# A spectral filter's coefficients laid out channel by channel: eviction into a staging tile, copies on POOL

## The chip, the cores and the metric

The kernel runs on one core of one Trainium2 chip. The metric is device time in microseconds of one execution: the median of several runs of the same kernel. A profiled execution gives the trace; it has a time of its own, and a span from its first to its last instruction.

Five engines work side by side, each on its own queue of instructions: PE (TensorE, the matrix multiplier; its weight loads are shown as PEld), DVE (VectorE), ACT (ScalarE), POOL (GpSimd) and SP, which here only issues DMAs. They meet in semaphores: an instruction adds to one when it is done, and another engine's queue waits until it has reached a count.

## What is computed

The input x is 32 images of 16 x 16 tokens with 32 channels, all in fp32. Four layers follow each other, each a pair of a mixing block and a feed-forward block on a normalised input, added back: linear attention and a spectral filter bank (layer 0), a triangle product and a recurrent cell (1), a row scan and a mixture of experts (2), a row scan and a recurrent cell (3). The change touches the filter bank of layer 0 and, in time, the attention that runs beside its preparation:

```python
def _stu_conv(phi, u, n):                      # u: (b, 256, 32), phi: (1024, 16)
    Vf = jnp.fft.rfft(phi, n=n, axis=0)
    Uf_p = jnp.fft.rfft(u, n=n, axis=1)
    Uf_m = jnp.fft.rfft(u * sgn3, n=n, axis=1)
    U_plus = jnp.fft.irfft(Vf[None, :, :, None] * Uf_p[:, :, None, :], n=n, axis=1)[:, :sl]
    U_minus = jnp.fft.irfft(Vf[None, :, :, None] * Uf_m[:, :, None, :], n=n, axis=1)[:, :sl]
    return U_plus, U_minus * sgn[None, :, None, None]
...
for i, frac in enumerate((1, 2, 4, 8)):        # the first T, T/2, T/4, T/8 tokens
    xi = x[:, :T // frac]
    si = einsum('btkd,k,kde->bte', U_plus, s, Mpp) + einsum('btkd,k,kde->bte', U_minus, s, Mpm) + ar(Mu, xi)
    outs.append(pad(si))
return jnp.sum(jnp.stack(outs, axis=-1) * weights, axis=-1)
```

## The kernel before

The program is written engine by engine: one function each for `sync`, `gpsimd`, `tensor`, `scalar` and `vector`, and the order of every queue is the order of the code. There is no scheduler. `S("name")` is a semaphore.

**Attention, 16 rounds.** `U = 16` pairs of a token chunk and an image group pass through a software pipeline. The loops `for i in range(U + 3)` on PE and ACT hold round i: ACT takes the exponential of the shifted q of unit i - 1 (`a_q`, L1226), the transposed k (`a_kn`, L1232), the exponential of k of unit i (`a_k`, L1211), then v (`a_v`, L1220). DVE turns the sum of the exponential of q into weights (L1534, L1536, L1539). POOL's `q_normalise(u)` (L591) multiplies exponential and weights of unit u; since the exponential of unit u comes in round u + 1, so does this product. Matmuls go through the helper `full` (L646).

**Filter turns.** Beside the rounds 6 to 13 the filters of the spectral bank are made, two turns a round: `filter_turn(i, part)` gives turn m = 2 (i - 6) + part, 16 in all. Turn m makes the output channels m and m + 16. PE writes them into banks 4 and 5 (`filters(m)`; it first waits for `filt_sb >= m`, the eviction of the turn before), and ACT evicts them in three instructions (`a_filters(m)`): short filters in time (L1240), spectra `w_f[1]` of the half-length filter on 64 partitions (L1242), and spectra `w_f[0]` of the full-length filter on 128 partitions (L1244). Each of the two spectra is 2 channels x 256 values: 128 frequencies, real and imaginary part. On ACT the first turn of a round lies ahead of `a_v`, the second behind it.

**How the spectra lie.** A partition is an input channel of a part of the filter. In the tiles `w_f` the 256 x 32 values of a partition are laid out as (n, e, i) with `FI = 8` values i of neighbouring frequencies side by side, then the 32 channels e, then the blocks n of frequencies. An eviction writes runs of 8 floats; a read of one frequency's 32 channels steps 8 floats.

**The filter stage.** After attention PE transforms the tokens, and `frequencies` multiplies, frequency by frequency: the weights are the spectrum of x at one frequency (32 columns, `x_fb`), the moving operand is 2 x 32 values of `w_fr`. A call has 128 such matmuls, four of them side by side on four column groups, and a matmul in fp32 leaves two records in the trace. The first call uses `w_f[0]`, the second `w_f[1]`. Between them stand `segment` (L846), which reads the Toeplitz tile `toep` that SP's DMAs fill out of the short filters, and `way_back` (L870), the inverse transform.

Of the kernel before, what the change touches and what calls it, by code (L numbers as in the profile page):

```python
# [21 lines left out]
P = 128  # L22
# [32 lines left out]
HT = T // 2  # L55
FREQ = HT
LAGS = T // 4
FI = 8
TRI_ORDER = [2, 3, 0, 1]
DFT_BANKS = [6, 7, 0, 1, 2, 5, 3, 7]  # L60

# [39 lines left out]
def build(nc, force_steps=False, **d):  # L101
    x, out = d["x"], d["out"]
    with ExitStack() as ctx:
# [64 lines left out]
        SEG_T = [None, None, T // 4, T // 8]  # L168
        SEG_AT = [None, None, 0, T // 4]
        toep = arena[:, AT_TOEP:AT_TOEP + N_TOEP].rearrange("p (t e) -> p t e", e=C)  # L170

# [368 lines left out]
        @block.sync  # L542
        def _(sp):
            def load(name, dst, src):
                sp.dma_start(dst, src).then_inc(S(name), 16)

            load_x(sp, 0, (0, 1))
            load("consts_in", consts[:, :], d["consts"])
            load_x(sp, 1, (0, 1))
            load("w_attn_in", w_attn[:, :], d["w_attn"])  # L550
            for to, rows in FILTER_ROWS:
                load("w_stu_in", w_stu[to:to + rows.stop - rows.start, :], d["w_stu"][rows, :])
            for to, rows in FILTER_ROWS:
                load("w_spec_in", wm_raw[to:to + rows.stop - rows.start, :, :].rearrange("p f m -> p (f m)"), d["w_spec"][rows, :])
            load("w_fft_in", arena[:, AT_FFT:AT_FFT + N_FFT], w_fft)
            load("w_late_in", w_late[:, :], d["w_late"])


            sp.wait_ge(S("filt_zero"), 1)
            sp.wait_ge(S("filt_sb"), C // 2)  # L560
            for n in (3, 2):
                for r in range(NQ):
                    sp.dma_start(toep[C * r:C * r + C, SEG_AT[n]:SEG_AT[n] + SEG_T[n], :],
                                 filt[C * n:C * n + C, AR - r:AR - r + SEG_T[n], :]).then_inc(S(f"toep{n}_in"), 16)
            sp.wait_ge(S("back_f"), 3)
            for par in range(2):
                load("w_moe", w1[64 * par:64 * par + C + 1, :, :],
                     d["w1"].rearrange("(e two) d h -> two d e h", two=2)[par])
            load("w_moe", w2[:, :, :], d["w2"][:, 0:HID, :].rearrange("e h o -> h e o"))
            store_first(sp, (0, 1))  # L570
            sp.wait_ge(S("y_final"), 2)
            store_last(sp, (0, 1))
            sp.wait_ge(S("stored"), 16 * 2 * NQ)
# [3 lines left out]
        def _(pool):  # L577
# [23 lines left out]
            for u in range(U):  # L601
                q_normalise(u)
                if 2 <= u < 2 + FRACS - 1:
                    pool.wait_ge(S("wm_scaled"), u)
                    link(pool.tensor_tensor(wm_raw[:, u - 1, :], wm_raw[:, u - 1, :], wm_raw[:, u - 2, :], ALU.add))
                if u == FRACS:
                    pool.sem_inc(S("wm_seg"), 1)


            pool.wait_ge(S("stu_ps"), 1)  # L610
# [31 lines left out]
        def _(pe):  # L642
# [234 lines left out]

            pe.wait_ge(S("x_f_act"), 4)
            pe.wait_ge(S("x_f_dve"), 4)
            frequencies(0, slice(0, P), w_fr[0])  # L880
            segment(2, 8, 16).then_inc(S("stu_ps"), 1)

# [284 lines left out]
        def _(act):  # L1167
# [70 lines left out]
            def a_filters(m):  # L1238
                act.wait_ge(S("filt_ps"), m + 1)
                act.activation(filt[2 * C:, AR:, m::C // 2].rearrange("p t e -> p e t"),  # L1240
                               bank[2 * C:, 4:6, 2 * FREQ:2 * FREQ + LAGS], ACT.Copy)
                act.activation(w_f[1][0:2 * C, m::C // 2, :, :],  # L1242
                               bank[0:2 * C, 4:6, 2 * FREQ:4 * FREQ].rearrange("p k (n i) -> p k n i", i=FI), ACT.Copy)
                act.activation(w_f[0][:, m::C // 2, :, :],  # L1244
                               bank[:, 4:6, 0:2 * FREQ].rearrange("p k (n i) -> p k n i", i=FI), ACT.Copy)\
                    .then_inc(S("filt_sb"), 1)

            for i in range(U + 3):
                if 0 <= i - 1 < U:
# [759 lines left out]
```

## Time and profile before

| | us |
|---|---|
| median of 3 runs (384.47 to 387.49) | 385.49 |
| profiled execution | 385.72 |
| its span, first to last instruction | 383.9 |
| PE busy | 346.4 |
| VectorE busy | 229.1 |
| ScalarE busy | 191.1 |
| POOL busy | 31.9 |

A sum over parts of the trace is made against the profiled execution's 385.72. Busy time is the sum of an engine's instructions; matmuls are pipelined, so PE's records overlap, and how fast PE works is read from the distance between starts. Rows of a timeline merge neighbours of one kind, with their count behind an x.

### The profile page before, as it was taken

The page shows a single profiled execution, that of the slowest core. Times are in us where ns is not written, and L with a number is a line of the kernel's source. Part 1 is how long each engine was busy: PE and PEld are TensorE (multiplying, and loading weights), DVE is VectorE, ACT ScalarE, POOL GpSimd, SP SyncE. Part 2 cuts the span into 40 slices and gives each one's busy share as a digit, 9 for nine tenths or more (in the row PEclk, how much of TensorE's full clock was granted, in tenths as well). Part 3 has the DMA queues.
Part 4 walks back from the last instruction along what each step waited for, and adds up shares of the span by engine and source line. Part 5 has one row for each costly group of instructions (what it writes and reads, how often), then busy time and mean ns, then how long its engine had stood idle before and what let it go on. Part 6 is the DMA issues. An engine that isn't in the chain of part 4 may idle for free.

```text
span 383.9 us, 9504 instructions
## 1 busy us (share of the span) xinstructions
PE 346.4 (90%) x4064; PEld 231.1 (60%) x4064; DVE 229.1 (60%) x461; ACT 191.1 (50%) x419; POOL 31.9 (8%) x37
## 2 busy tenths in 40 slices
PE   7967999999998999998988999799998899999990
PEld 2434555655645799974655369247746654773790
DVE  2679967767766522137846773762437366245884
ACT  1959678979748500026672646360247315033560
POOL 0024722121220000000000000000000000000000
PEclk9999999999999999999999999899999899999996
DMA  8982000000330000002000000000000000000004
GB/s 238 155 161 87 2 2 3 2 3 3 87 81 0 3 3 2 5 22 36 2 2 2 0 3 0 3 0 2 2 0 2 0 3 0 2 2 1 2 0 112
DMA packets 7338, 9.91 MB, mean 26 GB/s; under 512 B 3694, under 2 KB 6398, under 8 KB 6910
## 3 DMA queue, kind: packets, MB, share of 16 engines
q1 hardware_dynamic: 5630, 8.23, 10.3%
q10 hardware_dynamic: 1664, 1.05, 1.0%
q8 instruction: 33, 0.54, 0.6%
q14 instruction: 11, 0.09, 0.1%
HBM read 6.65 MB, written 1.05 MB: 20 GB/s over the span
## 4 chain that ended last, share of the span: by engine, by line
PE 64%; DVE 15%; ACT 13%; issue 5%; DMA 2%; SPq 0%; DVEq 0%; ACTq 0%
PE bank L646 28%; PE bank L1076 6%; PE bank L274 6%; PE bank L268 5%; PE bank L1006 4%; PE bank L1017 4%; PE bank L846 2%; ACT lnv L373 2%; PE bank L870 2%; DMA sb_consts<-in_consts 2%; ACT rs L378 2%; ACT arena L1242 1%; ACT arena L1244 1%; DVE arena L1771 1%; PE bank L1133 1%
## 5 line engine op out<-in xcount | busy, mean ns | idle before, releaser
L367 ACT ACTIVATE sq<-bank 128x512 f32<-128x512 f32 x33 | 19.4, 591 | 66.1 <-PE bank L268 50.7
L646 PE MATMUL bank<-xn,sb_w_attn 128*128 128x512 f32 x64 | 34.6, 622 | 6.8 <-ACT attn_scratch L1211 4.3
L646 PE MATMUL bank<-sb_consts 128*128 128x512 f32 (+1 forms) x84 | 37.4, 554 | 0.0
L274 PE MATMUL bank<-sq,sb_consts 128*128 128x512 f32 x66 | 34.7, 611 | 0.6 <-ACT sq L367 0.3
L373 ACT ACTIVATE lnv<-bank 128x512 f32<-128x512 f32 x33 | 19.7, 597 | 30.2 <-PE bank L274 29.9
L646 PE MATMUL bank<-arena 64*32 64x256 f32 (+4 forms) x466 | 26.7, 382 | 3.6 <-ACT arena L1244 2.2
L1076 PEld LDWEIGHTS bank<-arena,sb_w_late 128*128 128x128 f32 x180 | 23.0, 190 | 10.8 <-DVE arena L1829 7.6
L1017 PE MATMUL bank<-arena,sb_w_late 128*128 128x128 f32 x144 | 27.9, 276 | 0.0
L1006 PE MATMUL bank<-arena,sb_consts 128*128 128x128 f32 x144 | 27.7, 276 | 0.1
L1076 PE MATMUL bank<-arena,sb_w_late 128*128 128x128 f32 (+1 forms) x180 | 26.4, 283 | 1.4 <-DVE arena L1813 0.2
L1384 ACT ACTIVATE arena<-bank 128x128 f32<-128x128 f32 x72 | 20.0, 278 | 13.9 <-PE bank L1017 13.7
L646 PEld LDWEIGHTS bank<-arena 64*32 64x32 f32 (+3 forms) x466 | 17.4, 167 | 14.0 <-ACT arena L1244 8.2
L591 POOL TENSOR_TENSOR attn_scratch<-attn_scratch 128x512 f32<-128x512 f32 x16 | 20.4, 1275 | 62.4 <-DVE attn_scratch L1539 62.4
L646 PE MATMUL bank<-arena,attn_scratch 128*32 128x128 f32 (+2 forms) x768 | 24.0, 294 | 0.6 <-DVE attn_scratch L1584 0.6
L1829 DVE SCALAR_TENSOR_TENSOR arena<-bank,xn 128x128 f32<-128x128 f32 x30 | 8.8, 292 | 26.1 <-PE bank L1076 25.4
L646 PEld LDWEIGHTS bank<-arena,attn_scratch 128*32 128x32 f32 (+1 forms) x768 | 22.7, 129 | 1.9 <-DVE attn_scratch L1584 0.8
L1006 PEld LDWEIGHTS bank<-arena,sb_consts 128*128 128x128 f32 x144 | 21.7, 192 | 1.7 <-issue 1.7
L268 PE MATMUL bank<-xQ,sb_consts 128*128 128x512 f32 x40 | 20.9, 612 | 1.6 <-DMA sb_consts<-in_consts 1.4
L1017 PEld LDWEIGHTS bank<-arena,sb_w_late 128*128 128x128 f32 x144 | 21.9, 192 | 0.2
L378 ACT ACTIVATE rs<-lnv 128x512 f32<-128x512 f32 x33 | 20.8, 630 | 1.1
L646 PEld LDWEIGHTS bank<-sb_consts 128*128 128x128 f32 x84 | 14.7, 195 | 10.6 <-issue 10.4
L646 PEld LDWEIGHTS bank<-wvo,xn 128*128 128x128 f32 x128 | 16.1, 191 | 6.6 <-issue 6.6
(207 smaller groups left out, 622.3 us busy)
## 6 DMA issues: line engine op xcount, KB each, us to landing
arena<-in_w_spec SPq DMA_DIRECT2D x2, 720.0 KB
sb_w_late<-in_w_late SPq DMA_DIRECT2D x1, 1100.5 KB, 24.3
arena<-arena SPq DMA_DIRECT2D x4, 256.0 KB, 4.1
arena<-fourier SPq DMA_DIRECT2D x1, 768.0 KB, 22.0
sb_w_attn<-in_w_attn SPq DMA_DIRECT2D x1, 641.0 KB, 9.7
xR<-in_x SPq DMA_DIRECT2D x4, 128.0 KB, 3.9
xR<-in_x ACTq DMA_DIRECT2D x4, 128.0 KB, 4.1
arena<-in_w_spec SPq DMA_DIRECT2D x2, 256.0 KB
```

The lines of the kernel that those rows point to most:

```text
L268: pe.matmul(bank[:, centre_bank(i), :], centre, src, start=True, stop=True).then_inc(S("ln_centred"), 1)
L274: pe.matmul(bank[:, var_bank(i), :], mean32, sq[:, i % 2, :], start=True, stop=True)\
L367: act.activation(sq[:, i % 2, :], bank[:, centre_bank(i), :], ACT.Square).then_inc(S("ln_squared"), 1)
L373: act.activation(lnv[:, i % 2, :], bank[:, var_bank(i), :], ACT.Ln, bias=LN_EPS[norm_of(i)])\
L378: act.activation(rs[:, i % 2, :], lnv[:, i % 2, :], ACT.Exp, scale=-0.5).then_inc(S("ln_rstd"), 1)
L591: link(pool.tensor_tensor(qn[:, u % QN, :], qe[:, u % 2, :], qn[:, u % QN, :], ALU.mult))
L646: return mm(ps, lhsT, rhs, start=True, stop=True)
L1006: mm(place(s, h), ident, z_[:, h, s % RES, :, :], start=True, stop=False)
L1017: mm(place(s_, h), rvt[i], before(h, s_ % RES), start=False, stop=True)\
L1076: last = mm(bank[:, 4 + h % 2, B * lo:B * hi], band[i][:, w, :], carry[:, h - 1, w + lo:w + hi, :], start=(w == 1), stop=(w == 2), skip_gr ...
L1384: act.activation(y_[:, h, s_ % RES, 1:PASS + 1, :], bank[:, 4 + h + 2 * (s_ % 2), 0:PASS * HALF].rearrange("p (n g) -> p n g", g=HALF), AC ...
L1829: dve.scalar_tensor_tensor(out=carry[:, h, 1:5, :], in0=bank[:, 4 + h % 2, 0:P].rearrange("p (w b) -> p w b", b=B), scalar=0.0, in1=xn[:, ...
```

## The change

`FI` becomes 1: a frequency's 32 channels now lie side by side, and the values of one channel lie 32 floats apart. ScalarE no longer writes that layout. It evicts a turn's spectra in contiguous runs of 256 floats into a new staging tile `turned`, which has two slots (m % 2) and lies over the memory of the Toeplitz tile, unused at that time. POOL then copies a turn from its slot to its places in `w_f`, `w_f[1]` first, one instruction each, and counts them in the new semaphore `spectra` (two a turn). Three waits on it are new: ScalarE before it fills a slot again (turn m waits until turn m - 2 has been copied), SP before the DMAs that fill the Toeplitz tile, and PE before the first `frequencies`. The core of the diff:

```diff
-FI = 8
+FI = 1
...
+        turned = arena[:, AT_TOEP:AT_TOEP + 2 * 2 * 4 * FREQ].rearrange("p (w m k n) -> p w m k n", w=2, m=2, k=2)
...
             sp.wait_ge(S("filt_sb"), C // 2)
+            sp.wait_ge(S("spectra"), C)
             for n in (3, 2):
...
                 if u == FRACS:
                     pool.sem_inc(S("wm_seg"), 1)
+                for m in filter_turn(u, 0) + filter_turn(u, 1):
+                    pool.wait_ge(S("filt_sb"), m + 1)
+                    for w_ in (1, 0):
+                        to = slice(0, 2 * C if w_ else P)
+                        pool.tensor_copy(w_f[w_][to, m::C // 2, :, :],
+                                         turned[to, w_, m % 2, :, :].rearrange("p k (n i) -> p k n i", i=FI))\
+                            .then_inc(S("spectra"), 1)
...
             pe.wait_ge(S("x_f_dve"), 4)
+            pe.wait_ge(S("spectra"), C)
             frequencies(0, slice(0, P), w_fr[0])
...
-                act.activation(w_f[1][0:2 * C, m::C // 2, :, :],
-                               bank[0:2 * C, 4:6, 2 * FREQ:4 * FREQ].rearrange("p k (n i) -> p k n i", i=FI), ACT.Copy)
-                act.activation(w_f[0][:, m::C // 2, :, :],
-                               bank[:, 4:6, 0:2 * FREQ].rearrange("p k (n i) -> p k n i", i=FI), ACT.Copy)\
-                    .then_inc(S("filt_sb"), 1)
+                if m >= 2:
+                    act.wait_ge(S("spectra"), 2 * (m - 1))
+                act.activation(turned[0:2 * C, 1, m % 2, :, :], bank[0:2 * C, 4:6, 2 * FREQ:4 * FREQ], ACT.Copy)
+                act.activation(turned[:, 0, m % 2, :, :], bank[:, 4:6, 0:2 * FREQ], ACT.Copy).then_inc(S("filt_sb"), 1)
```

Two places show what that makes of the queues; an entry's brackets hold the semaphores that it waits for. The first is ScalarE's queue in one round with two filter turns, before:

```order
L1226 ACTIVATE attn_scratch<-attn_scratch 128x512 [waits q_norm,q_shift]
L1232 ACTIVATE attn_scratch<-bank 128x512 [waits ctx_ps,k_tr]
L1211 ACTIVATE attn_scratch<-bank,attn_scratch 128x256 [waits k_tr,k_max]
L1211 ACTIVATE attn_scratch<-bank,attn_scratch 128x256
L1240 ACTIVATE arena<-bank 64x2x64 [waits filt_ps]
L1242 ACTIVATE arena<-bank 64x2x32x8
L1244 ACTIVATE arena<-bank 128x2x32x8
L1220 ACTIVATE attn_scratch<-bank 128x512 [waits ctx_ps,v_ps]
L1240 ACTIVATE arena<-bank 64x2x64 [waits filt_ps]
```

And the same round after the change (lines are shifted by 11 here: L1226 is now L1237, and L1240, L1242, L1244 are L1251, L1255, L1256):

```order
L1237 ACTIVATE attn_scratch<-attn_scratch 128x512 [waits q_norm,q_shift]
L1243 ACTIVATE attn_scratch<-bank 128x512 [waits ctx_ps,k_tr]
L1222 ACTIVATE attn_scratch<-bank,attn_scratch 128x256 [waits k_tr,k_max]
L1222 ACTIVATE attn_scratch<-bank,attn_scratch 128x256
L1251 ACTIVATE arena<-bank 64x2x64 [waits filt_ps]
L1255 ACTIVATE arena<-bank 64x512 [waits spectra]
L1256 ACTIVATE arena<-bank 128x512
L1231 ACTIVATE attn_scratch<-bank 128x512 [waits ctx_ps,v_ps]
L1251 ACTIVATE arena<-bank 64x2x64 [waits filt_ps]
```

The instructions are the same in number and place; the second eviction of a turn has got the wait for `spectra`, and the destination is no longer cut into pieces of 8. The second place is POOL's queue from the last segment sum (L605) through the products of q to the first memset of the triangle block, before:

```order
L591 TENSOR_TENSOR attn_scratch<-attn_scratch 128x512 [waits q_weight,pool_step]
L605 TENSOR_TENSOR arena<-arena 128x1024 [waits pool_step,wm_scaled]
L591 TENSOR_TENSOR attn_scratch<-attn_scratch 128x512 [waits pool_step,q_weight] x11
L612 MEMSET arena 128x32x16 [waits pool_step,stu_ps]
L612 MEMSET arena 128x32x16 [waits pool_step]
```

And after the change, from the products of units 5 and 6 to the first copy behind the product of unit 7:

```order
L594 TENSOR_TENSOR attn_scratch<-attn_scratch 128x512 [waits pool_step,q_weight] x2
L615 COPY arena<-arena 64x2x256 [waits pool_step,filt_sb]
L615 COPY arena<-arena 128x2x256
L615 COPY arena<-arena 64x2x256 [waits filt_sb]
L615 COPY arena<-arena 128x2x256
L594 TENSOR_TENSOR attn_scratch<-attn_scratch 128x512 [waits q_weight]
L615 COPY arena<-arena 64x2x256 [waits pool_step,filt_sb]
```

Eight of the products now have four copies behind them: those of turns 2 (u - 6) and 2 (u - 6) + 1 stand behind the product of unit u, which waits for `q_weight`.

## Rows read from the trace of the kernel before

**Rows 1.** The page's first part: busy time, share of the span, instructions.

```profile
PE 346.4 (90%) x4064; PEld 231.1 (60%) x4064; DVE 229.1 (60%) x461; ACT 191.1 (50%) x419; POOL 31.9 (8%) x37
```

**Rows 2.** Timeline of ScalarE (ACT) in two rounds: start, us, instruction, [idle before it].

```profile
61.74 0.62 ACT L1226 ACTIVATE attn_scratch<-attn_scratch 128x512 f32<-128x512 f32 x1
...
63.78 0.39 ACT L1240 ACTIVATE arena<-bank 64x128 f32<-64x128 f32 x1
64.18 0.59 ACT L1242 ACTIVATE arena<-bank 64x512 f32<-64x512 f32 x1
64.67 0.58 ACT L1244 ACTIVATE arena<-bank 128x512 f32<-128x512 f32 x1
65.27 0.60 ACT L1220 ACTIVATE attn_scratch<-bank 128x512 f32<-128x512 f32 x1
66.56 0.38 ACT L1240 ACTIVATE arena<-bank 64x128 f32<-64x128 f32 x1 [0.69 <-PE bank L646]
...
67.92 0.62 ACT L1226 ACTIVATE attn_scratch<-attn_scratch 128x512 f32<-128x512 f32 x1
...
77.03 0.58 ACT L1244 ACTIVATE arena<-bank 128x512 f32<-128x512 f32 x1
```

**Rows 3.** Timeline of PE in the same two rounds.

```profile
65.30 0.90 PE L646 MATMUL bank<-arena 64*32 64x256 f32 x20 [0.17 <-ACT arena L1244]
...
77.29 1.09 PE L646 MATMUL bank<-attn_scratch 128*32 128x256 f32 x16
78.31 0.90 PE L646 MATMUL bank<-arena 64*32 64x256 f32 x20
```

**Rows 4.** Timeline of PE from 128 to 171 us, the filter stage.

```profile
128.02 2.01 PE L355 MATMUL bank<-xQ,sb_consts 128*32 128x128 f32 x32
129.84 1.95 PE L646 MATMUL bank<-arena,attn_scratch 128*32 128x128 f32 x64
...
136.40 2.48 PE L846 MATMUL bank<-xn,arena 128*128 128x256 f32 x16
138.81 8.18 PE L646 MATMUL bank<-arena,attn_scratch 128*32 128x64 f32 x256
146.92 5.94 PE L846 MATMUL bank<-xn,arena 128*128 128x256 f32 x32
152.79 3.76 PE L870 MATMUL bank<-arena,attn_scratch 128*32 128x128 f32 x128
156.47 8.18 PE L646 MATMUL bank<-arena,attn_scratch 64*32 64x64 f32 x256
...
167.51 3.10 PE L870 MATMUL bank<-arena,attn_scratch 128*32 128x64 f32 x128
170.54 1.12 PE L274 MATMUL bank<-sq,sb_consts 128*128 128x512 f32 x2
```

**Rows 5.** Timeline of VectorE (DVE) in the round from 61.74.

```profile
63.43 0.71 DVE L1539 STREAM_TRANSPOSE attn_scratch<-attn_scratch 128x512 f32<-128x512 f32 x1
```

**Rows 6.** Timeline of POOL.

```profile
21.79 0.62 POOL L596 TENSOR_SCALAR sb_w_stu<-sb_w_stu,sig 128x128 f32<-128x128 f32 x1 [20.20 <-ACT odd_sig L1186]
...
36.72 2.36 POOL L605 TENSOR_TENSOR arena<-arena 128x1024 f32<-128x1024 f32 x1 [0.18 <-POOL attn_scratch L591]
...
64.22 1.28 POOL L591 TENSOR_TENSOR attn_scratch<-attn_scratch 128x512 f32<-128x512 f32 x1 [4.90 <-DVE attn_scratch L1539]
...
152.92 1.14 POOL L612 MEMSET arena<- 128x512 f32 x2 [39.41 <-PE bank L846]
```

**Rows 7.** Timeline of PE at 24 us.

```profile
23.88 1.10 PE L646 MATMUL bank<-xn,sb_w_attn 128*128 128x512 f32 x2 [2.60 <-ACT attn_scratch L1211]
```

**Rows 8.** Stretches around 244 us; length, busy us of each engine, granted clock (PEclk).

```profile
241.00:244.40 3.40, 1.83 (x10) 0.87 (x8) 2.20 (x7) 0.81 (x3) 0.00 (x0) 1.00 0.00 0
244.50:247.80 3.30, 2.76 (x13) 0.55 (x16) 2.02 (x4) 1.80 (x2) 0.00 (x0) 0.50 0.04 10
```

**Rows 9.** Timeline of SP's DMA queue from 90 to 130 us.

```profile
100.22 6.07 SPq L563 DMA_DIRECT2D arena<-arena  x8
```

## The prediction

> **What bounds the kernel now.** I read the page first: PE is busy for 90% of the span, so most stages are paced by PE or by an engine that PE waits for [rows 1]. Then I read the two stages that the change touches, in order of time.
>
> The attention rounds, 50 to 100 us. The order of work has eight rounds that each carry two filter turns. I take the round in which ScalarE starts L1226 at 61.74; the next one starts at 67.92, so a round lasts 6.18 us [rows 2]. ScalarE works nearly all of it; it idles once, 0.69 us, before the eviction of the second turn. PE shows why: its second turn (65.30) waits for ScalarE's L1244, the eviction of the first turn [rows 3]. So ScalarE's list of work plus one hop over PE is the round, and a delay in front of L1242 moves everything behind it. POOL does one product of 1.28 us in a round and is idle for the rest.
>
> The filter stage, 128 to 172 us. PE runs without a break there, and the two `frequencies` calls last 146.92 - 138.81 = 8.11 us and, with the same 8.18 us of records, as much again from 156.47 on [rows 4]. Time saved in them is saved in the span; the transposes and adds on VectorE that follow start when they end, and move along.
>
> **The matmuls that read the spectra.** A call has 256 records of 64 columns, so one takes 31.7 ns. Its moving operand today steps 8 floats from channel to channel; after the change it is contiguous. The number of instructions stays. What a step costs is seen in rows of the same 32-column weights: L355 reads 128 columns at a step of 4 floats in (129.84 - 128.02)/32 = 56.9 ns, the contiguous transforms behind it take 1.95/64 = 30.5 ns for as many columns [rows 4]. For 64 contiguous columns the row is L870 at 167.51: (170.54 - 167.51)/128 = 23.7 ns. By it a call takes 6.06 us and both calls gain 4.1 us. I take this value, since shape and weights are nearest. The other ends: if columns alone set the pace, half of L870's 128-column pace, (156.47 - 152.79)/128/2 = 14.4 ns, gives 8.9 us; if loading the strided weights sets the 31.7 ns, the gain is 0.
>
> **ScalarE's own time.** Three evictions a turn remain three. L1244 took 0.58 us into runs of 8 floats, and L1220 took 0.60 for the same size into contiguous memory [rows 2]. So the new form gains nothing there; I take 0.
>
> **The new wait.** From turn 2 on ScalarE stands before its second eviction until POOL has copied turn m - 2. Behind it in ScalarE's queue are the rest of the turn, the eviction of v, and the second turn; PE's second turn waits for the first one's end. The point is where POOL does that copy. Its queue has the copies of a round's two turns behind that round's product, and that product needs weights which VectorE can only make from ScalarE's L1226 in the next round. So in the round from 61.74 the copies of the earlier round's first turn come behind the product that starts at 64.22, which starts 0.08 us after VectorE's L1539 ends (63.43 + 0.71) [rows 5, 6]. The product ends at 65.50; POOL's next instruction behind a product followed by 0.18 us at 36.72 [rows 6]; then come two copies of c each, and a hop to ScalarE that I price like the 0.08 us from VectorE. ScalarE wants L1242 at 64.18 [rows 2]. The stall is 65.50 + 0.18 + 2c + 0.08 - 64.18 = 1.58 + 2c.
>
> This happens in the seven rounds that wait in their first turn (m = 2, 4, ... 14). The product starts within 0.05 us of L1242 in all of them, since both follow from L1226. In one of them (first turn at 76.13 to 77.61) PE is busy with the attention output from 77.29 to 78.31 when L1244 ends at 77.03 + 0.58 = 77.61, so 0.65 us of the stall is covered there [rows 2, 3]. The second turn of a round waits for two copies more; it comes 2.8 us later in ScalarE's queue (66.56 + 0.39 against 64.18), so it adds nothing while 2c is below that.
>
> The trace has no copy on POOL, so c has to be bounded. Below: a memset of the same 512 elements, which only writes, 1.14/2 = 0.57 us. Above: the product, with two reads, 1.28 us for 512 elements [rows 6]. A copy has one read and one write, here with a step of 128 bytes; I take the middle, 0.92 us. The stall is 3.42 us, and 7 x 3.42 - 0.65 = **23.3 us** are lost; with 0.57 it is 18.4, with 1.28 it is 28.3.
>
> The Trainium skill (GPSIMD Engine Reference, section 3.1) gives 769 ns for 512 elements in its best loop, measured with a tight body. With an estimate of 0.77 from that page the loss would be 21.2 us and the forecast about 2 us lower. No row here shows a copy, and the page's pitfalls list a price for reads with large steps only, not for writes.
>
> **PE's clock in the stalls.** Today PE waits 0.17 us in a round; then it will wait some 3.6 us in one piece. The longest idle time before 370 us is 2.60 us (ahead of 23.88), and the clock was held through it [rows 7]. But from 241.00 to 244.40, where PE was busy for 1.83 us of 3.40, the clock was granted in full, and right behind it, from 244.50 to 247.80, it was 0.50, the lower of the two levels [rows 8]. So longer waits can bring the lower level. What would stand on the path at 1.2 GHz is the second turn's work on PE up to ScalarE's next start, 66.56 - 65.30 = 1.26 us, once more per round; the rest of the round's matmuls lies beside ScalarE and the next stall. Seven rounds are 8.8 us; I take half, 4.4.
>
> **What costs nothing.** The eight DMAs of the Toeplitz tile on SP (from 100.22, 6.07 us) now wait for POOL's last copy. It stands behind the product of the round after the last turn: 2.48 (from L1226 to the product) + 1.28 + 0.18 + 4c = 7.6 us into that round. PE needs their tile at 136.40, at the first L846, and before that it waits for nothing of it [rows 4, 9]. PE's own new wait ahead of 138.81 is over by then. The last two products on POOL come when it has long caught up.
>
> **Sum.** Against the profiled execution (385.72 us, 0.23 above the median of the runs): + 23.3 + 4.4 - 4.1 = + 23.6, so 409.3, or 409 beside the median of 385.49.
>
> **Rivals.**
> 1. The clock falls in all seven stalls. 23.3 + 8.8 - 4.1 = + 28.0, 413.7. For it: the new gaps are longer than any that the trace shows held. Against it: around each gap PE is busy without a break. The Trainium skill (TensorE: Matmul & The Clock Gate, HAM oscillation) describes just this, idle gaps between bursts that bring the lower clock at every one; rows 7 and 8 show one case each way.
> 2. The matmuls gain nothing, since the strided weights of 32 columns set their pace. + 27.7, 413.4. Against it: the pair of rows at 128.02 and 129.84, where the step alone nearly doubles the time.
> 3. POOL is far slower with steps. Its TENSOR_SCALAR on 128 elements with a step of 2 took 0.62 us [rows 6]; four times that is 2.5 us a copy. The stall is 6.6 us, the second turn waits 2.2 us more (2c - 2.8), and 7 x 8.8 - 0.65 + 4.4 - 4.1 = + 61.3, 447. Against it: that instruction also takes a scalar per partition, and its fixed part is counted four times.
> 4. The other side: the wait is hidden and only PE's gain is left, 385.72 - 4.1 = 381.6 (376.8 with 8.9). This needs POOL to be through with turn m - 2 when ScalarE comes to L1242. It decides at a stall of 4.1/7 = 0.59 us a round (1.27 with the larger gain); the part without any copy, 1.58, is above both. So the product would have to start a full microsecond earlier beside L1226, or the copies would have to run ahead of it, and the order of POOL's queue says that they don't.
>
> **Chances and range.** Forecast 0.57, rival 1 0.20, rival 2 0.09, rival 3 0.09, rival 4 0.05. Lower end: c = 0.57, no fall of the clock, gain 8.9: + 9.5, 395. Upper end: c = 1.28, all falls of the clock, no gain: + 37.1, 423. That holds the forecast and rivals 1 and 2, and leaves out 3 and 4. The runs before spread over 0.8%, so about 1% is what a measurement can tell from no change. Faster by over 1%: 0.03; within 1%, where a small stall meets the gain: 0.03; slower: 0.94.
>
> **What would show it.** In the changed profile: ScalarE's second eviction (now L1255) idle 3 to 4 us in seven rounds, put down to POOL, with rounds of 9 to 10 us between starts of the exponential of q; POOL's copies at 0.6 to 1.3 us each, right behind each product; PE idle some 3.6 us ahead of a round's second turn, and its granted clock in tenths below 9 in those slices if it falls; the two `frequencies` calls at 6 us each. I am wrong if POOL's copies stand ahead of the product in time, if ScalarE doesn't wait for them, or if the calls shrink by more than the rounds grow.

## The result, and the profile after

The changed kernel takes 413.08 us (median of 4 runs, 410.43 to 414.11) beside 385.84 for the kernel before on the same chip: a ratio of 1.0695, 95% interval 1.065 to 1.0739. It is slower by 27 us; the forecast was 409 in a range of 395 to 423. The profiled execution took 412.96, its span 411.1, so 27.2 more than the span before.

The page of the changed kernel: busy time, the granted clock in 40 slices, and the chain of work that ended last.

```profile
PE 356.1 (87%) x4064; PEld 229.5 (56%) x4064; DVE 228.9 (56%) x461; ACT 191.1 (46%) x419; POOL 62.9 (15%) x69
...
PEclk9989998696968999996999999999999989999997
...
PE 59%; DVE 17%; ACT 10%; issue 6%; POOL 6%; DVEq 0%; ACTq 0%; POOLq 0%
```

ScalarE is busy for the same 191.1 us as in [rows 1]; POOL has 31 us more work. POOL now stands in the chain with 6%, and the clock has dents, four of them between 60 and 120 us, where the attention rounds lie. (PE's busy time rises because records at the lower clock last longer; [rows 3] had 0.90 us for the 20 records that take 1.54 below.)

Two rounds of ScalarE's timeline answer to [rows 2]. The lines have moved: L1226, L1240, L1242, L1244 and L1220 are now L1237, L1251, L1255, L1256 and L1231.

```profile
65.17 0.62 ACT L1237 ACTIVATE attn_scratch<-attn_scratch 128x512 f32<-128x512 f32 x1
...
67.88 0.40 ACT L1251 ACTIVATE arena<-bank 64x128 f32<-64x128 f32 x1 [0.50 <-PE bank L656]
71.29 0.59 ACT L1255 ACTIVATE arena<-bank 64x512 f32<-64x512 f32 x1 [3.02 <-POOL arena L615]
...
75.88 0.62 ACT L1237 ACTIVATE attn_scratch<-attn_scratch 128x512 f32<-128x512 f32 x1
...
80.02 0.39 ACT L1251 ACTIVATE arena<-bank 64x128 f32<-64x128 f32 x1 [1.24 <-PE bank L656]
82.32 0.59 ACT L1255 ACTIVATE arena<-bank 64x512 f32<-64x512 f32 x1 [1.91 <-POOL arena L615]
...
86.06 0.62 ACT L1237 ACTIVATE attn_scratch<-attn_scratch 128x512 f32<-128x512 f32 x1
```

A round that took 6.18 us takes 10.71 and 10.18. The second eviction waits for POOL once a round, and where the clock is low, the first one already waits for PE. Over the whole program the groups of these two lines (busy, mean ns, then idle time before them) say how much; the last row is the first eviction in the kernel before:

```profile
L1255 ACT ACTIVATE arena<-bank 64x512 f32<-64x512 f32 x16 | 9.4, 590 | 19.7 <-POOL arena L615 19.6
...
L1251 ACT ACTIVATE arena<-bank 64x128 f32<-64x128 f32 x16 | 6.2, 389 | 15.3 <-PE bank L656 15.2
...
L1240 ACT ACTIVATE arena<-bank 64x128 f32<-64x128 f32 x16 | 6.2, 388 | 8.2 <-PE bank L646 8.0
```

So 19.6 us of waiting for POOL are new, and 7.2 of the 15.2 for PE; 8.0 were there before.

POOL's timeline in the first of these waits, which answers to [rows 6], and its two groups of copies:

```profile
57.18 1.26 POOL L594 TENSOR_TENSOR attn_scratch<-attn_scratch 128x512 f32<-128x512 f32 x1 [7.00 <-DVE attn_scratch L1549]
58.62 3.89 POOL L615 COPY arena<-arena 64x512 f32<-64x512 f32 x4 [0.17 <-POOL attn_scratch L594]
```

```profile
L615 POOL COPY arena<-arena 128x512 f32<-128x512 f32 x16 | 17.3, 1079 | 0.0
L615 POOL COPY arena<-arena 64x512 f32<-64x512 f32 x16 | 17.0, 1062 | 1.3 <-POOL attn_scratch L594 1.3
```

The copies stand right behind the product, 0.17 us later, and four of them take 3.89 us, 0.97 each. PE's second turns, which answer to [rows 3], and two neighbouring stretches with PE's granted clock (length, busy us of PE, PEld, DVE, ACT and POOL, clock):

```profile
72.42 1.54 PE L656 MATMUL bank<-arena 64*32 64x256 f32 x20 [3.19 <-ACT arena L1256]
...
83.45 0.91 PE L656 MATMUL bank<-arena 64*32 64x256 f32 x20 [2.07 <-ACT arena L1256]
```

```profile
71.80:78.60 6.80, 6.18 (x40) 2.64 (x40) 2.11 (x4) 4.36 (x12) 1.29 (x2) 0.50 0.01 2
78.60:85.40 6.80, 4.73 (x107) 3.17 (x107) 2.58 (x6) 2.85 (x8) 5.24 (x5) 1.00 0.01 2
```

PE idles 2 to 4 us ahead of the second turn in each of the seven rounds. Behind the idle piece that ended at 72.42 the clock is at its lower level, 1.2 GHz, until 78.60; the same 20 records last 1.54 us there and 0.91 at 2.4 GHz. Then comes the filter stage, which answers to [rows 4]:

```profile
167.94 4.10 PE L656 MATMUL bank<-arena,attn_scratch 128*32 128x64 f32 x246
172.96 0.40 PE L656 MATMUL bank<-arena,attn_scratch 128*32 128x64 f32 x10 [0.92 <-issue]
173.29 5.94 PE L856 MATMUL bank<-xn,arena 128*128 128x256 f32 x32
...
182.85 3.69 PE L656 MATMUL bank<-arena,attn_scratch 64*32 64x64 f32 x214
187.78 1.40 PE L656 MATMUL bank<-arena,attn_scratch 64*32 64x64 f32 x42 [1.24 <-issue]
189.11 1.93 PE L656 MATMUL bank<-attn_scratch,sb_consts 128*32 128x128 f32 x32
...
197.73 1.12 PE L276 MATMUL bank<-sq,sb_consts 128*128 128x512 f32 x2
```

The two calls of `frequencies` take 5.35 and 6.26 us instead of 8.11 and 8.12. But each has a pause, 0.92 and 1.24 us, in which PE waits for nothing that the profile shows, and behind the second pause the clock is at its lower level for a while: the 32 records from 189.11 take 1.93 us, 1.08 before.

The account, by starts of ScalarE's exponential of q and of PE's rows, before and after:

| stretch | before | after | difference |
|---|---|---|---|
| start to first waiting round (55.55, 54.69) | 55.55 | 54.69 | -0.86 |
| seven rounds (to 100.03, 127.47) | 44.48 | 72.78 | +28.30 |
| to the first transform of the tokens (126.25, 155.37) | 26.22 | 27.90 | +1.68 |
| filter stage, to the row at 170.54, 197.73 | 44.29 | 42.36 | -1.93 |
| the rest | 213.4 | 213.4 | 0.0 |

The first line lies before anything that the change touches: PE's row of [rows 7] already starts at 23.00 instead of 23.88. This account is of one execution of each kernel.

### The profile page after: what moved, and what is told of

Read it like the earlier page. It is cut to its first block, busy times and chain, and to the rows that moved or that the text cites. A ratio compares the mean times of both kernels' runs of the same rounds, so it can differ in the third digit from the quotient of the medians.

```text
span 411.1 us, 9536 instructions
## 1 busy us (share of the span) xinstructions
PE 356.1 (87%) x4064; PEld 229.5 (56%) x4064; DVE 228.9 (56%) x461; ACT 191.1 (46%) x419; POOL 62.9 (15%) x69
## 4 chain that ended last, share of the span: by engine, by line
PE 59%; DVE 17%; ACT 10%; issue 6%; POOL 6%; DVEq 0%; ACTq 0%; POOLq 0%
PE bank L656 25%; PE bank L1087 6%; PE bank L276 6%; PE bank L270 5%; PE bank L1017 4%; PE bank L1028 3%; POOL arena L615 3%; POOL attn_scratch L594 2%; PE bank L856 2%; ACT lnv L375 2%; PE bank L880 2%; DVE attn_scratch L1544 2%; ACT rs L380 1%; DVE attn_scratch L1549 1%; ACT arena L1256 1%
## 5 line engine op out<-in xcount | busy, mean ns | idle before, releaser
L656 PE MATMUL bank<-arena 64*32 64x256 f32 (+4 forms) x466 | 29.4, 428 | 21.8 <-ACT arena L1256 20.4
L656 PE MATMUL bank<-xn,sb_w_attn 128*128 128x512 f32 x64 | 42.4, 751 | 5.4 <-ACT attn_scratch L1222 3.2
L656 PE MATMUL bank<-sb_consts 128*128 128x512 f32 (+1 forms) x84 | 38.3, 567 | 0.0
L656 PEld LDWEIGHTS bank<-arena 64*32 64x32 f32 (+3 forms) x466 | 16.9, 166 | 35.4 <-ACT arena L1256 23.8
L1526 DVE TENSOR_REDUCE attn_scratch<-bank 128x2 f32<-128x512 f32 x16 | 11.0, 687 | 43.3 <-PE bank L656 43.3
L615 POOL COPY arena<-arena 64x512 f32<-64x512 f32 (+1 forms) x32 | 31.0, 1070 | 1.3 <-POOL attn_scratch L594 1.3
L270 PE MATMUL bank<-xQ,sb_consts 128*128 128x512 f32 x40 | 22.7, 662 | 0.2 <-DVE xQ L1726 0.2
```

The source lines that it names most:

```text
L270: pe.matmul(bank[:, centre_bank(i), :], centre, src, start=True, stop=True).then_inc(S("ln_centred"), 1)
L615: pool.tensor_copy(w_f[w_][to, m::C // 2, :, :], turned[to, w_, m % 2, :, :].rearrange("p k (n i) -> p k n i", i=FI))\
L656: return mm(ps, lhsT, rhs, start=True, stop=True)
```

## The experiments

The theory: the rounds are longer because a slot is waited for whose copies stand behind this round's product in POOL's queue, the clock adds to that, and the matmuls' gain is small beside it. The rivals: POOL is simply too slow for copies of this form; the clock's falls are hidden; and, for the filter stage, what takes back the gain.

**Copies ahead of the product.** The changed kernel, with POOL's loop turned round:

```diff
             for u in range(U):
-                q_normalise(u)
...
                 for m in filter_turn(u, 0) + filter_turn(u, 1):
                     pool.wait_ge(S("filt_sb"), m + 1)
...
+                q_normalise(u)
```

> The changed kernel with one block moved: POOL's copies of a round's two turns stand ahead of the product of the same unit instead of behind it; slots, copies, waits are the same. Order theory (the stall is the place of the copies behind a product that can only come in the next round): the copies run in the second half of a round and are over about 0.4 us before the product wants to start, ScalarE doesn't wait for POOL, rounds are back at 6.2 us, PE's clock stays at the upper level in the rounds. From the changed kernel that takes 28.3 us off the rounds and 1.7 off the stretch behind them: about 383 us. Throughput rival (two products' worth of strided copying a round is too much for POOL, or its copies disturb VectorE): rounds stay above 8 us and the time above 400.

Measured: 382.11 us, ratio to the kernel before 0.9926 (0.9899 to 0.9953). Rounds of 6.17 to 6.19 us in six of the seven, as before the change, and no wait of ScalarE for POOL. POOL's timeline:

```profile
58.88 2.07 POOL L609 COPY arena<-arena 64x512 f32<-64x512 f32 x2 [0.17 <-POOL attn_scratch L594]
61.31 2.01 POOL L609 COPY arena<-arena 64x512 f32<-64x512 f32 x2 [0.36 <-ACT arena L1256]
63.63 1.28 POOL L594 TENSOR_TENSOR attn_scratch<-attn_scratch 128x512 f32<-128x512 f32 x1 [0.30 <-DVE attn_scratch L1549]
```

The same copies, as slow as before (4 in 4.1 us), fill 5.4 us of POOL's round of 6.2 together with the product, and cost nothing: with two slots, it is the order that makes the stall.

**Four slots.** The order of the queue stays, but a slot is waited for two rounds later:

```diff
-                if m >= 2:
-                    act.wait_ge(S("spectra"), 2 * (m - 1))
-                act.activation(turned[0:2 * C, 1, m % 2, :, :], bank[0:2 * C, 4:6, 2 * FREQ:4 * FREQ], ACT.Copy)
+                if m >= 4:
+                    act.wait_ge(S("spectra"), 2 * (m - 3))
+                act.activation(turned[0:2 * C, 1, m % 4, :, :], bank[0:2 * C, 4:6, 2 * FREQ:4 * FREQ], ACT.Copy)
```

> The changed kernel with four slots in the staging tile instead of two; POOL's order stays. Order theory: a slot is free a whole round earlier (ScalarE waits for turn m - 4), so the late copies no longer hold ScalarE: rounds of 6.2 us, the same 383 us as with the copies ahead of the product. Throughput rival: as there, rounds above 8 us, since POOL does not get through whatever the number of slots.

Measured: 381.76 us, ratio 0.9913 (0.9886 to 0.9939), the same rounds, no wait for POOL, though its copies stand behind the product as in the changed kernel. The rival of a POOL that is too slow is out.

**Three slots**, between the two:

> The changed kernel with three slots in the tile between ScalarE and POOL, instead of two (413.1) or four (381.8). Theory of order: what counts is whether the copies that a slot waits for stand in POOL's queue ahead of the product that waits for this round's exponential, or behind it. With three, the first turn of a round waits for copies of the round before the last, long done, and the second turn for the first two copies behind this round's product, which end about 0.5 to 0.7 us after ScalarE gets there: no wait on the first, 0.5 to 0.7 on the second, rounds of 6.7 to 6.9 us, and 385 to 387 us in all. Rival, each slot fewer costs the same share of the stall: half of it, about 397.

The edit is as above, with `m % 3`, `m >= 3` and `2 * (m - 2)`. Measured: 386.25 us, ratio 1.0027 (0.9993 to 1.0061), inside the interval of the order theory. ScalarE's timeline in one round:

```profile
63.93 0.59 ACT L1255 ACTIVATE arena<-bank 64x512 f32<-64x512 f32 x1
...
67.46 0.59 ACT L1255 ACTIVATE arena<-bank 64x512 f32<-64x512 f32 x1 [0.76 <-POOL arena L615]
```

The first turn waits for nothing, the second 0.76 to 0.83 us in each round, a little over the 0.5 to 0.7 expected, and six of the seven rounds take 6.94 to 7.00 us. One of the two added slots takes away 27 of 31 us, as the order says, and not half of them.

**The same layout as before, with the copies.** `FI` stays 8, everything else is as in the changed kernel:

```diff
-FI = 1
+FI = 8
```

> The changed kernel with FI = 8 again: staging and POOL's copies as in the change, but the old layout, so that the matmuls gain nothing. Order theory with a copy that costs the same in runs of 8: the rounds as in the changed kernel (72.8 us for seven), the two calls of frequencies at 8.1 us again without a pause of PE and without the fall of the clock behind the second: 413.0 + 2.0, about 415. If the step of 128 bytes is what makes a copy take 0.95 us, copies of runs of 8 would be near the memset's 0.57 and the stall 0.8 us shorter: about 409.

Measured: 406.58 us, ratio 1.0569 (1.0516 to 1.0622). The copies in runs of 8 floats:

```profile
L615 POOL COPY arena<-arena 128x512 f32<-128x512 f32 x16 | 9.7, 607 | 0.0
L615 POOL COPY arena<-arena 64x512 f32<-64x512 f32 x16 | 9.7, 604 | 1.3 <-POOL attn_scratch L594 1.3
```

0.61 us instead of 1.08: the step of 128 bytes costs POOL 0.47 us a copy. ScalarE's wait for POOL falls from 19.6 to 15.3 us, not to zero: four copies take 2.27 us in a round, 0.57 each, and 1.58 + 2 x 0.57 = 2.72 is what ScalarE waits there (2.69 at 60.18). The 1.58 are the product's place and do not depend on the copies. The calls of `frequencies` are back at 8.05 us and have no pause. The time is 2.4 us below the second expectation; 1.8 of them lie behind the filter stage, where nothing was changed (211.6 us for what took 213.4).

**ScalarE writes the new layout itself.** The kernel before, with one number changed and no copies:

```diff
-FI = 8
+FI = 1
```

> The kernel before with FI = 1 alone: ScalarE evicts straight into the new layout, single floats 128 bytes apart, no staging tile, no POOL. It prices what the copies stand for. If ScalarE's evictions keep their 0.59 and 0.58 us, the rounds stay at 6.2 us and the time is that of the matmuls' gain alone, about 383 us. If ScalarE pays for the step as POOL's copies do (0.95 us against 0.57 for a memset of the same size), two evictions a turn cost 0.4 us more each, 4 in a round, eight rounds: + 12 us, about 395.

Measured: 394.20 us, ratio 1.0231 (1.018 to 1.0281). The two evictions of spectra, here and then with `FI = 8`, are 1.08 and 1.06 against 0.58 and 0.59 us, and a round takes 7.8 us:

```profile
L1244 ACT ACTIVATE arena<-bank 128x512 f32<-128x512 f32 x16 | 17.3, 1082 | 0.0
L1242 ACT ACTIVATE arena<-bank 64x512 f32<-64x512 f32 x16 | 16.9, 1059 | 0.2
```

The price of the step is real on ScalarE too: its seven rounds are 10.7 us longer than before, against 28.3 with the detour over POOL.

**Layouts between**, again written by ScalarE alone: the kernel before with `FI = 4`, and with `FI = 2`.

> The kernel before (385.5) with runs of 4 channels instead of 8 in the filter spectra: ScalarE writes straight to their places, in runs of 16 bytes, and a matmul of frequencies reads its 64 columns at a step of 16 bytes instead of 32; no POOL copies. Known so far: at runs of 8 an eviction takes 0.58 to 0.59 us and a matmul 31.7 ns; with the channels side by side 1.06 to 1.08 us and 16.4 ns. If the price of a read goes by the bytes that it spans, the matmuls pace at 16 to 24 ns, a call takes 5 to 6.3 us; if only side by side is fast, 31.7 and 8.1. If the price of a write goes by the pieces it is cut into, an eviction takes about 0.65 to 0.75 us, rounds 6.4 to 6.8 us; if any step over 32 bytes costs all of it, 1.07 and rounds of 7.8 us. By the first of each the time is 383 to 386, by the second of each 396 to 398.

> The kernel before with runs of 2 channels' neighbours: ScalarE writes straight to their places in runs of 8 bytes, a matmul of frequencies reads its 64 columns at a step of 8 bytes. At runs of 8 and of 4 (385.5, 385.3 us) an eviction took 0.58 to 0.59 us and a matmul 31.3 to 31.7 ns; at runs of 1 (394.2) 1.06 to 1.08 us and 16.4 ns. Theory A, both prices belong to elements that lie apart at all: evictions 0.58, matmuls 31.5, rounds 6.2, calls 8.0 each, 385 us. Theory B, both go by bytes per line, so that runs of 2 lie on the way: evictions 0.7 to 0.8, matmuls 20 to 24 ns, rounds 6.6 to 6.9, calls 5.1 to 6.2 with little pause: 384 to 387. If reads gain and writes don't pay: rounds 6.2, calls 4.2 to 6.2, 381 to 383.

Measured: 385.34 us with 4 (ratio 0.9986, 0.9952 to 1.002) and 384.14 with 2 (0.9962, 0.9929 to 0.9995). With 4 the evictions are those of 8 (0.58, 0.59 us), and the calls nearly so (7.95 us each, 8.11 and 8.12 before). So the reads behave as in the second case of that expectation and the writes as in neither, and the time lies in the first interval by another road. With 2, the evictions and the first call:

```profile
L1242 ACT ACTIVATE arena<-bank 64x512 f32<-64x512 f32 x16 | 9.8, 610 | 0.2
L1244 ACT ACTIVATE arena<-bank 128x512 f32<-128x512 f32 x16 | 9.6, 600 | 0.0
```

```profile
138.55 4.20 PE L646 MATMUL bank<-arena,attn_scratch 128*32 128x64 f32 x246
143.60 0.40 PE L646 MATMUL bank<-arena,attn_scratch 128*32 128x64 f32 x10 [0.85 <-issue]
```

Reads at a step of 8 bytes run at 4.20/246 = 17.1 ns a record, as good as the contiguous ones' 4.10/246 = 16.7, and writes in runs of 8 bytes cost 0.02 us more than runs of 32. Neither theory A nor B holds, but the last of the three cases, with a time 1 us above it: both prices are jumps and not slopes, and `FI = 2` lies on the good side of both. With it the kernel before gets both paces by one digit, and no copy. In time that is little, 0.4%, and not more than four slots gave with the copies (ratio 0.9913; the two intervals overlap a little). Its profiled execution took 380.31 us; the other nine lie at 381.3 to 384.8.

**PE kept busy in the wait.** The changed kernel, with matmuls that nobody reads ahead of a round's second turn, seven and then two:

```diff
                 for m in filter_turn(i, 1):
+                    if m >= 2:
+                        pe.wait_ge(S("k_rows"), i)
+                        keep_busy(7, 3)
                     filters(m)
```

> The changed kernel (413.1 us) with seven matmuls of 512 columns that nobody reads (1.5 us at the full clock) ahead of the second turn's matmuls from the second round on, where TensorE otherwise waits 2.1 to 4.2 us for ScalarE. The stall itself, ScalarE waiting for POOL's copies, is untouched. Theory: of the 28.3 us that the seven rounds are longer, about 4.3 are the clock falling in every second round, and some 1.7 more its fall just behind them; with the gap filled the clock stays at its higher level, the rounds take 9.6 to 9.8 us each and the time is 406 to 408.5. Rival: all of the 28.3 us is the stall, and a slower TensorE is hidden behind it: the clock rises to 0.97 or more, and the time stays at 412 to 414.

Measured: 423.70 us, ratio 1.0991 (1.0932 to 1.105), outside both expectations. My size for a filler was wrong: one matmul of 512 columns leaves two records of 0.45 us, so seven took 6.28 us, more than the wait, and became the round, 11.6 to 12.2 us in six of the seven. The clock held in all seven rounds, but the run cannot tell what that is worth.

> e6_fillers_in_wait again with two matmuls ahead of the second turn in place of seven. There the seven took 6.28 us, since one of 512 columns runs as two records of 0.45 us, and filled more than the wait of 2.1 to 4.2 us; two take 1.8 us and fit into it. Theory: the clock keeps its higher level in the rounds, they take 9.5 to 9.9 us each instead of 10.4, and the time is 406 to 409.5. Rival, a slower TensorE is hidden behind the stall: the clock rises and the time stays at 412 to 414.

Measured: 408.67 us, ratio 1.0586 (1.0524 to 1.0648), so 4.4 less than the changed kernel. The wait for POOL is the same:

```profile
62.28 0.59 ACT L1258 ACTIVATE arena<-bank 64x512 f32<-64x512 f32 x1 [3.49 <-POOL arena L615]
```

```profile
69.33 1.98 PE L656 MATMUL bank<-sb_consts 128*128 128x512 f32 x4
73.05 0.90 PE L656 MATMUL bank<-arena 64*32 64x256 f32 x20 [1.74 <-ACT arena L1259]
```

The seven rounds take 69.41 us instead of 72.78, with one fall of the clock left (at 102.85), and the two intervals behind them 9.74 instead of 11.41, as before the change (9.73). Rounds without a fall take 9.66. The stall alone is 9.66 - 6.18 = 3.48 us, and the clock's falls are on the path beside it. (The one round without a fall in the changed kernel, from 97.11, took 9.69, so the two fillers themselves add nothing to a round.)

**The pause in the calls.** Four slots, and matmuls that nobody reads inside each call, two and then one:

```diff
                 for n in range(FREQ // NQ):
+                    if n == 24:
+                        keep_busy(2, 7 if k0 == 0 else 3)
                     for k in range(NQ):
```

> Four slots as in e2_four_slots (381.8 us), and two matmuls of 512 columns that nobody reads, put into each of the two calls of frequencies after 100 of its 256 pairs. If the pause in each call (0.70 and 1.03 us there, put to issue) is TensorE's instructions arriving late, the two matmuls (0.43 us of work, one of them in place of two short ones' worth of instructions) fill a part of it: the calls stay at about 5.9 us each, the pauses shrink by about 0.4 each, the clock no longer falls behind the second call, and the time is 379 to 381. If the pause is a fixed stop whatever runs ahead of it, each call is 0.43 us longer, the pauses and the fall behind them stay, and the time is 382 to 383.5.

Measured: 382.37 us, ratio 0.991 (0.988 to 0.9939). Two fillers took 1.98 us and not 0.43, the same slip as above. The pauses are gone and the clock no longer falls behind the second call, but the calls take 6.23 and 6.36 us, against 5.11 and 5.54 with four slots alone, and the time lies in the interval of the other case.

> e5_fillers_in_calls with one matmul of 512 columns in each call instead of two. There two took 1.98 us, the pauses went and the clock no longer fell behind the second call, but the calls were 1.12 and 0.82 us longer than in e2_four_slots, which is as much as was won behind them. One takes 0.99, about what the pauses were (0.70 and 1.03). If the pause is the supply of instructions, which a filler feeds for as long as it runs, the calls are 0.1 to 0.4 us longer than in e2_four_slots, the pauses go, the clock does not fall behind the second call, and the time is 379.8 to 381.2 against 381.8. If the pause is only shifted, the pauses stay at 0.7 to 1.0 us, and the time is 382 to 383.5.

Measured: 380.58 us, ratio 0.9895 (0.985 to 0.9939). The stage with four slots alone, and then with one filler:

```profile
153.49 3.64 PE L656 MATMUL bank<-arena,attn_scratch 64*32 64x64 f32 x214
158.16 0.94 PE L656 MATMUL bank<-arena,attn_scratch 64*32 64x64 f32 x42 [1.03 <-issue]
159.03 1.94 PE L656 MATMUL bank<-attn_scratch,sb_consts 128*32 128x128 f32 x32
...
163.48 3.05 PE L880 MATMUL bank<-arena,attn_scratch 128*32 128x64 f32 x128
```

```profile
153.86 3.60 PE L656 MATMUL bank<-arena,attn_scratch 64*32 64x64 f32 x192
157.38 1.12 PE L656 MATMUL bank<-sb_consts 128*128 128x512 f32 x2
...
159.23 0.97 PE L656 MATMUL bank<-arena,attn_scratch 64*32 64x64 f32 x46 [0.22 <-issue]
160.12 1.08 PE L656 MATMUL bank<-attn_scratch,sb_consts 128*32 128x128 f32 x32
...
163.05 2.98 PE L882 MATMUL bank<-arena,attn_scratch 128*32 128x64 f32 x128
```

The time is where the first case had it, but not by its road: the pauses shrink to 0.54 and 0.22 us instead of going, and the calls are 6.20 and 6.26 us long, 1.1 and 0.7 more than without the filler instead of 0.1 to 0.4. What is won lies behind: from the end of the second call to the next `way_back` (L880, L882) it takes 2.93 us instead of 4.45, since the clock holds. In time the filler is not clear of four slots alone (0.9895 beside 0.9913, and the first interval holds the second). With one filler or two a call takes 6.2 to 6.4 us, so the fillers do not only fill time that was lost.

> e8_direct_fi2 (384.1 us; no POOL copies, matmuls of frequencies at a step of 8 bytes) with one matmul of 512 columns in each call, as in e11_filler_in_calls. In the profiled execution of e8 the pauses were 0.85 and 1.16 us and no fall of the clock stood behind them, and that execution was its fastest, 380.3; its other nine lie at 381.3 to 384.8. If what sets these apart is the clock falling behind the second call, as it does in the profiles of the changed kernel and of e1 and e2, the filler holds it and the median comes to 379.5 to 381.5, with little spread. If the spread has another cause, the filler costs 0.7 to 1.1 us a call and gives nothing back: 384 to 386.

Measured: 381.71 us, ratio 0.9906 (0.987 to 0.9941). The edit is `FI = 2` in the kernel before and the filler. The calls take 5.50 and 6.50 us, with pauses of 0.23 and 0.15 in the second:

```profile
155.42 2.00 PE L646 MATMUL bank<-arena,attn_scratch 64*32 64x64 f32 x108 [0.23 <-issue]
157.35 1.12 PE L646 MATMUL bank<-sb_consts 128*128 128x512 f32 x2
158.41 0.58 PE L646 MATMUL bank<-arena,attn_scratch 64*32 64x64 f32 x18
159.15 0.98 PE L646 MATMUL bank<-arena,attn_scratch 64*32 64x64 f32 x46 [0.15 <-issue]
```

The time is 0.2 above the expected interval; the median of `FI = 2` fell by 2.4 us (from ratio 0.9962 to 0.9906, with intervals that overlap a little), and the nine runs lie at 379.93 to 383.57, so most of the spread is still there. That the clock behind the second call made the slower runs of `FI = 2` is likely by this, not shown: only one execution of each has a trace.

## Why the prediction was right

**The stall** (predicted 23.3): right in place, cause and size. It was derived as 1.58 + 2c a round, with c = 0.92 for a copy. The copies came at 0.97 each, which makes 3.52, and where the clock held, rounds grew by 3.48 us (two fillers in the wait). Seven of them with the covered one (10.27 against 7.39 in that round) are 23.8 us. (In the changed kernel itself ScalarE waits only 19.6 us for POOL, since a turn that a fall of the clock has made late comes later to the slot.) That the middle of two bounds came so near to c is partly luck: in runs of 8 floats a copy takes 0.57 us, the lower bound itself, and the rest is the step, which no row before could price. That the order of POOL's queue is the cause was shown from both sides: the same copies ahead of the product, or the same order with four slots, cost nothing; and with cheaper copies 15.3 us of wait remain. Rival 4 named what would have turned the sign, copies ahead of the product; built so, the kernel took 382.1, 3.1 below the kernel before beside it (385.2), where that rival said 4.1.

For c, the Trainium skill (GPSIMD Engine Reference, section 3.1) has 0.769 us for 512 elements, which was weighed and not taken. A copy here lasts 0.60 to 0.61 in runs of 8 floats and 1.06 to 1.08 at a step of 128 bytes, one below that figure and one above, so the measured ones stand.

**The clock** (predicted 4.4, half of seven falls): right in the rounds, 28.30 - 23.8 = 4.5 us, for four falls. With two fillers 3.4 of it came back and one fall stayed. The half was a hedge between two outcomes and not derived, so that four of seven came is luck. [rows 7] could not have decided it: the same 2.60 us of idle time stand ahead of 23.00 in the changed kernel's profile, and from 24.50 to 27.00 the clock is 0.50 there and 1.00 in the kernel before (the dent in the third slice of the page). Of the fourteen profiles of this document eight have that early fall and six have not, so one execution does not say what the clock makes of a wait. What I did not foresee is its reach: the fall at 126.4, at the end of the last round, added 1.68 us where nothing waits for POOL, and the same fillers removed it. Rival 1, a fall in every round, gave 413.7, by chance nearer to the 413.1 measured; the trace has four in the seven rounds and this one.

**The matmuls' gain** (predicted -4.1, ends -8.9 and 0): here the step failed in size. Two things were wrong in opposite directions. The pace: I took the row of L870 (L880 after the change), 23.7 ns for 64 contiguous columns, as nearest; the records run at 4.10/246 = 16.7 ns, near the 14.4 that I had as the bound by columns. By that pace alone a call would take 4.3 us and both gain 7.7. But the calls shortened by 2.76 and 1.86, 4.6 in sum, because of the pauses; and the clock's fall behind the second gave back 2.67 (the rows from 189.11 to 197.73 took 8.62 us, the same work before 5.95). Net -1.93. I had no term for a supply of instructions or for a fall of the clock after a gain.

What the pause is: most likely PE's instructions arriving late. The page counts 33 loads on the instruction queue, 0.54 MB, for 8128 records of PE, so one load of 16 KB carries about 246 of them, 123 weight loads and as many matmuls. In the changed kernel one such load starts in the first call (40 slices from 170.0 to 174.0 us, 0.1 us each, GB/s):

```profile
GB/s 0 0 0 0 0 164 0 0 0 0 0 0 0 0 0 0 0 0 0 0 0 0 0 0 0 0 0 0 0 0 0 0 0 0 0 0 0 0 0 0
...
q8 instruction: 1, 0.02, 1.4%
```

It starts at 170.5 to 170.6, and PE goes on at 172.96, 2.4 us later; in the second call one starts at 185.4 to 185.5, and PE goes on at 187.78. At 31.7 ns a record, 123 matmuls last 3.9 us, and the next load is there in time; at 16.7 they last 2.1 and it is not.

The place of the pauses speaks for it too: it goes by the count of instructions and not by what they do. Without a filler they come behind 246 records of the first call and 214 of the second. With one filler, two records, the first comes behind 192 + 2 + 52 = 246 and the second behind 192 + 2 + 18 = 212, since the stream has moved on by the first call's two. And where the second call pauses twice (`FI = 2` with a filler), 108 + 2 + 18 = 128 matmul records lie between, with their weight loads (one for each, 4064 of either on the page) 256 instructions. The Trainium skill (Advanced Engine Details and Errata, Sequencer and Instruction Queues) describes an instruction cache with lines of 16 KB, 256 instructions; the trace agrees with both numbers. No run changed the loading itself, so this is inferred, not shown. Two things stay open: the pauses of 0.92 and 1.24 us are longer than 2.4 - 2.1 makes them, and why a filler does not shorten the calls. With one the load itself starts later, 3.4 us into the first call (141.4 to 141.5) instead of 2.4 with four slots alone (141.2 to 141.3); what sets a load off no run shows.

**The sum.** 28.3 + 1.7 - 1.9 - 0.9 = 27.2 us against 23.6 forecast. Of the 3.6 between them 2.2 are the matmuls' term, 1.7 the fall behind the rounds, 0.6 the stall and the clock in the rounds, and 0.9 the other way lie ahead of the change. The terms at nothing held: ScalarE's evictions took 0.59 and 0.58 us as in [rows 2], and the tail and SP's DMAs moved nothing.

## What to carry to other kernels

A staging buffer between two engines is as deep as the order of the consumer's queue makes it: find the instruction that stands ahead of the consumer in its queue, and ask which round that one waits for; here two more slots or a loop turned round were worth 31 us, while a copy nearly twice as fast, with the old layout, left 21 us of loss. Before staging a change of layout, look for the smallest run that satisfies both sides: with 2 floats side by side reader and writer were both fast, with no copy at all, and no faster in time than copies that nobody waits for. And a gain on PE is counted only after asking what feeds it and what its clock does next.

## What the runs showed of the hardware

The price of a step is a jump. For reads it lies between a step of 16 bytes and one of 8, for writes between pairs of floats and single ones (all in fp32; reads in the first call):

| run of floats, step of a read | write of 512 floats by ScalarE, us | read, ns a record of 64 columns |
|---|---|---|
| 8, 32 bytes | 0.58 to 0.59 | 31.7 |
| 4, 16 bytes | 0.58 to 0.59 | 31.1 |
| 2, 8 bytes | 0.60 to 0.61 | 17.1 |
| 1, contiguous read, write at 128 bytes | 1.06 to 1.08 | 16.7 |

The Trainium skill (Advanced Engine Details and Errata, Memory Cachelines) says that SBUF has lines of 16 bytes and needs two hits on one to hide its latency. The table agrees with both numbers: reads at a step of 8 bytes, two to a line, are fast, and at 16 bytes, one to a line, slow; single floats written apart are slow, pairs are not. POOL pays as ScalarE does at the two ends that were run: 0.60 to 0.61 us in runs of 8 floats, 1.06 to 1.08 at single ones.
